# Masked cross-attention: the last key's term once per group, and weights and values as fp16 halves

## What is computed

```python
q = split_heads(layernorm(x) @ Wq + bq)        # 16 heads of 16
k = split_heads(ctx @ Wk + bk); v = split_heads(ctx @ Wv + bv)
scores = einsum('bhqd,bhkd->bhqk', q, k) / sqrt(16)
scores = where(mask > 0, -1e9, scores)         # mask is 1 on valid keys
p = softmax(scores)                            # over 257 keys
x = x + einsum('bhqk,bhkd->bhqd', p, v) @ Wo + bo
```

## Time and profile before

| | |
|---|---|
| median of 3 runs | 3067.11 us (3064.57 to 3067.53) |
| the profiled execution's own time | 3058.71 us |
| its span, first to last instruction | 3056.9 us |
| PE / DVE / ACT / POOL busy, share of the span | 86% / 66% / 59% / 54% |
| mean granted TensorE clock | 0.926 |

### The profile page before, as it was taken

One profiled execution on the slowest core, in us unless ns is written; L12 is line 12 of the kernel. 1 busy time (PEld: TensorE's weight loads), 2 busy tenths in 40 slices (PEclk: granted clock), 3 DMA queues, 4 the chain that ended last, 5 costly groups with the idle time before them and its releaser, 6 DMA issues. The chain is left out here.

```text
span 3056.9 us, 81164 instructions
## 1 busy us (share of the span) xinstructions
PE 2633.2 (86%) x31182; PEld 2052.3 (67%) x31182; DVE 2019.7 (66%) x4510; ACT 1814.4 (59%) x4252; POOL 1652.4 (54%) x1589
## 2 busy tenths in 40 slices
PE   2999999999985988986797999999994888527998
PEld 2888888888863655553355888888873666416776
DVE  4677777777764777776346777777766888653443
ACT  2667767667666777772345777777763666343333
POOL 3666666666635777773006666666644777142332
PEclk9999999999996999887798999999996999558999
DMA  5333332223300000000002212221200000451110
GB/s 145 85 84 85 84 82 76 75 77 84 92 28 1 1 1 1 1 1 14 16 15 84 64 49 64 64 64 49 64 18 16 2 2 2 170 181 48 38 40 26
DMA packets 120951, 160.04 MB, mean 52 GB/s; under 512 B 11456, under 2 KB 107840, under 8 KB 118400
## 3 DMA queue, kind: packets, MB, share of 16 engines
q1 hardware_dynamic: 115904, 140.28, 16.1%
q0 software_dynamic: 4672, 14.57, 1.3%
HBM read 139.99 MB, written 14.83 MB: 51 GB/s over the span
## 5 line engine op out<-in xcount | busy, mean ns | idle before, releaser
L570 ACT ACTIVATE x_prob<-x_prob,x_nm 128x257 f32<-128x257 f32 x512 | 254.5, 499 | 212.7 <-DVE x_nm L656 212.7
L1894 DVE TENSOR_TENSOR_SCAN m_s<-m_a,m_psD 128x1024 f32<-128x1024 f32 x128 | 284.9, 2267 | 3.0 <-PE m_psD L1721 2.9
L656 DVE CUSTOM_DVE_ANT_0 x_prob<-x_psS,x_masked,x_lastv 128x256 f32<-128x256 f32 x512 | 217.3, 481 | 104.0 <-PE x_psS L476 100.7
L1195 DVE SCALAR_TENSOR_TENSOR x_pTl<-x_psS,x_pTh 128x1024 f16<-128x1024 f32 x128 | 156.7, 1225 | 144.9 <-ACT x_pTh L1103 144.9
L1833 ACT ACTIVATE m_a<-m_dt,m_rate 128x248 f32<-128x248 f32 x512 | 206.9, 493 | 0.0
L2778 ACT ACTIVATE e1t_g<-e1t_psH,e1t_bias 128x128 f32<-128x128 f32 x312 | 89.2, 368 | 171.1 <-PE e1t_psH L2727 171.1
L1605 POOL TENSOR_TENSOR m_s<-m_s 128x1024 f32<-128x1024 f32 x64 | 150.6, 2354 | 68.5 <-DVE m_s L1894 68.5
L883 POOL TENSOR_TENSOR x_qbdh<-x_qh,all_mask4h 128x1024 f16<-128x1024 f16 x32 | 60.6, 1894 | 215.8 <-DVE x_ql L1176 215.8
L1116 ACT ACTIVATE x_vh<-x_psV 128x512 f16<-128x512 f32 x128 | 76.4, 597 | 134.4 <-PE x_psV L922 134.4
L875 POOL TENSOR_TENSOR x_ctxl<-x_ctx,x_ctxh 128x512 f16<-128x512 f32 x128 | 149.7, 1170 | 10.7
L318 POOL TENSOR_TENSOR x_ctxl<-x_ctx,x_ctxh 128x512 f16<-128x512 f32 x128 | 148.3, 1159 | 10.7
(11 more groups left out here) (591 smaller groups left out, 10617.9 us busy)
## 6 DMA issues: line engine op xcount, KB each, us to landing
x_ctx<-in_ctxT SPq DMA_DIRECT2D x64, 1024.0 KB, 6.2
x_mraw<-in_mask SPq DMA_DIRECT2D x128, 128.5 KB, 6.0
x_vxr<-x_vx SPq DMA_DIRECT2D x32, 512.0 KB, 6.9
e1r_stage<-in_L_ffn_w SPq DMA_DIRECT2D x16, 1024.0 KB, 5.0
e_rows<-e1r_pad POOLq DMA_DIRECT2D x1, 5070.0 KB, 19.6
e1t_row<-e_rows SPq DMA_DIRECT2D x39, 130.0 KB, 2.1
all_xres<-in_x SPq DMA_DIRECT2D x1, 4096.0 KB, 14.4
x_vxr<-x_vx SPq DMA_DIRECT2D x128, 32.0 KB, 3.5
```

What stands on the lines that cost most here:

```text
L570: last = act.activation(prob[b % NP][:, s, :], prob[b % NP][:, s, :], ACT.Exp, bias=nm[b % NP][:, s:s + 1], scale=-1.0, accum_out=sm[b // ...
L656: dve.tensor_tensor_reduce(prob[b % NP][:, s, 0:LAST], psS[:, s * LAST:(s + 1) * LAST], masked[g % 2][:, j, :], -SC, lastv[g % 2][:, j, s: ...
L1195: dve.scalar_tensor_tensor(pT[c % 4][1][:].rearrange("p r k n -> p (r k n)"), psS[c % 2][:], PS, pT[c % 4][0][:].rearrange("p r k n -> p ( ...
L1894: dve.tensor_tensor_scan(states, rates, psD[at % 2][:], 0.0, ALU.mult, ALU.add).then_inc(scan_done, 1)
```

## The change

Values and weights are written as fp16 pairs: ACT takes the high halves (`hi_v`; `hi_pT` now takes all 1024 columns of `psT`, scaled by `PS` = 4096), DVE the low halves (`lo_v`, `lo_pT`), which read both PSUM and the high half. `lo_v(b-1)` stands at the head of DVE's slot, `lo_pT(b-1)` where `take_pT(b-1)` stood. `attend` makes three fp16 products in place of one fp32 product. The last key's term leaves `attend`: POOL only sets its weights aside (`take_last`), spreads a group's weights in a second instruction like the one for the sums (`lasts`), PE sums them over heads in `denominators`, and DVE multiplies by the last key's values (`vx`, now transposed and kept in SBUF) and adds, in `normalise`. The DRAM round trip of those values and its broadcast loads are gone. Declarations, renames of semaphores and the unchanged surroundings are left out:

```diff
 sync
-            def load_vx(g):
-                wait(sync, pv_last, (g - 1) * GB)
-                src = vx_dram[g * GB:(g + 1) * GB, :].rearrange("(a j) n -> a j n", a=1).to_broadcast([P, GB, D])
-                sync.dma_start(vxr[g % 2][:], src).then_inc(vxr_in[g % 2], 16)
 gpsimd
-            def value_last(b):
-                g, j = b // GB, b % GB
+            def take_last(b):
                 pool.wait_ge(exp_done, b + 1)
-                pool.wait_ge(vxr_in[g % 2], 16 * (g // 2 + 1))
-                wait(pool, pv_mm, b - 2)
-                pool.tensor_tensor(pv32[b % 3][:].rearrange("p (c r n) -> p c r n", c=C, r=RG),
-                                   vxr[g % 2][:, j, :].rearrange("p (c r n) -> p c r n", c=C, r=RG),
-                                   strips(prob[b % NP][:, :, LAST]).unsqueeze(3).to_broadcast([P, C, RG, 64]), ALU.mult)\
-                    .then_inc(pv_last, 1)
+                pool.tensor_copy(plast[b // GB % 2][:, b % GB, :], prob[b % NP][:, :, LAST]).then_inc(taken, 1)
 
             def spread_sums(g):
                 pool.wait_ge(share_done, g + 1)
...
+                pool.wait_ge(taken, (g + 1) * GB)
+                pool.tensor_tensor(lasts[:], eye_q[:].unsqueeze(1).unsqueeze(1).to_broadcast([P, 4, GB, T]),
+                                   plast[g % 2][:].rearrange("p j s -> p s j").unsqueeze(3).to_broadcast([P, 4, GB, T]),
+                                   ALU.mult).then_inc(lasts_done, 1)
...
-                batch(value_last, b - 1)
+                batch(take_last, b - 1)
 tensor
             def denominators(g):
                 pe.wait_ge(sums_done, g + 1)
+                pe.wait_ge(lasts_done, g + 1)
                 wait(pe, q_lo, min(g + 3, NT))
-                for r in range(RG):
-                    last = pe.matmul(psA[64 * r:64 * r + 64, :], head_rows[:],
-                                     sums[:, 2 * r:2 * r + 2].rearrange("p c j t -> p (c j t)"), start=True, stop=True)
+                for to, src in ((0, sums), (256, lasts)):
+                    for r in range(RG):
+                        last = pe.matmul(psM[64 * r:64 * r + 64, to:to + 256], head_rows[:],
+                                         src[:, 2 * r:2 * r + 2].rearrange("p c j t -> p (c j t)"), start=True, stop=True)
...
-                wait(pe, v_out, b)
+                wait(pe, v_lo, b)
...
             def turn(b):
                 pe.wait_ge(exp_done, b + 1)
-                wait(pe, pt_first, b)
-                wait(pe, pt_second, b)
+                wait(pe, pt_lo, b)
...
             def attend(b):
-                pe.wait_ge(v_out, b + 1)
-                pe.wait_ge(pt_first, b + 1)
-                pe.wait_ge(pt_second, b + 1)
-                pe.wait_ge(pv_last, b + 1)
+                pe.wait_ge(v_lo, b + 1)
+                pe.wait_ge(pt_lo, b + 1)
...
-                        for r in range(RG):
-                            s = r * C + c
-                            pe.matmul(psO[64 * r:64 * r + 64, to:to + P],
-                                      V[b % NV][:, kt, c * P + 64 * r:c * P + 64 * r + 64], pT[b % NW][:, kt, s * P:(s + 1) * P],
-                                      start=b % 2 == 0 and kt == 0 and c == 0, stop=False, skip_group_check=True)
-                for c in range(C):
-                    to = (c * 2 + b % 2) * P
-                    for r in range(RG):
-                        last = pe.matmul(psO[64 * r:64 * r + 64, to:to + P],
-                                         pv32[b % 3][:, c * P + 64 * r:c * P + 64 * r + 64], con["ident"][:],
-                                         start=False, stop=True, skip_group_check=True)
+                        for v, p in ((0, 0), (0, 1), (1, 0)):
+                            for r in range(RG):
+                                s = r * C + c
+                                last = pe.matmul(psO[64 * r:64 * r + 64, to:to + P],
+                                                 V[b % NV][v][:, kt, c * P + 64 * r:c * P + 64 * r + 64],
+                                                 pT[b % NW][p][:, kt, s * P:(s + 1) * P],
+                                                 start=b % 2 == 0 and kt == 0 and c == 0 and (v, p) == (0, 0),
+                                                 stop=kt == 1 and (v, p) == (1, 0), skip_group_check=True)
 scalar
-                act.activation(pT[b % NW][:, 0, :], psT[:, 0:512], ACT.Copy).then_inc(pt_first, 1)
+                act.activation(flat(pT[b % NW][0]), psT[:], ACT.Copy, scale=PS).then_inc(pt_hi, 1)
 vector
-            def take_pT(b):
-                dve.wait_ge(t_mm, b + 1)
+            def lo_pT(b):
+                dve.wait_ge(pt_hi, b + 1)
                 wait(dve, pv_mm, b - NW + 1)
-                dve.tensor_copy(pT[b % NW][:, 1, :], psT[:, 512:1024]).then_inc(pt_second, 1)
+                dve.scalar_tensor_tensor(flat(pT[b % NW][1]), psT[:], PS, flat(pT[b % NW][0]), ALU.mult, ALU.subtract)\
+                    .then_inc(pt_lo, 1)
...
+            def lo_v(b):
+                dve.wait_ge(v_hi, b + 1)
+                wait(dve, pv_mm, b - NV + 1)
+                dve.tensor_tensor(flat(V[b % NV][1]), psV[:], flat(V[b % NV][0]), ALU.subtract).then_inc(v_lo, 1)
...
                 dve.wait_ge(o_ext, 2 * g + 2)
+                dve.wait_ge(vx_done, 1)
+                dve.tensor_tensor(term[:].rearrange("p c j t -> p (c j) t"), psM[:, 256:512].rearrange("p (n t) -> p n t", t=T),
+                                  vx[:, g].rearrange("p c j -> p (c j)").unsqueeze(2).to_broadcast([P, C * GB, T]), ALU.mult)\
+                    .then_inc(term_done, 1)
+                dve.wait_ge(term_done, g + 1)
                 row = oT[g % 2][:].rearrange("p c j t -> p (c j t)")
+                dve.tensor_tensor(row, row, term[:].rearrange("p c j t -> p (c j t)"), ALU.add).then_inc(term_added, 1)
+                dve.wait_ge(term_added, g + 1)
                 dve.tensor_tensor(row, row, psA, ALU.mult).then_inc(o_norm, 1)
...
+                batch(lo_v, b - 1)
                 batch(minima, b)
...
-                batch(take_pT, b - 1)
+                batch(lo_pT, b - 1)
```

More of the change, by code:

```diff
@@ L202, in masked_attention @@
         (kxp,) = parts("kx", [P, C, RG, NB], 1)
-        vx32 = sb("vx32", [P, D], F32)
-        vxr = [sb(f"vxr{n}", [P, GB, D], F32) for n in range(2)]
+        vx = sb("vx", [P, NT, C, GB], F32)
         mraw = sb("mraw", [P, GB, S2], I32)
@@ L212, in masked_attention @@
         qbd = parts("qbd", [P, C, GB, 4, T], 2)
-        K, V = parts("k", [P, C, LAST], NK), [sb(f"v{n}", [P, 2, D], F32) for n in range(NV)]
+        K, V = parts("k", [P, C, LAST], NK), parts("v", [P, 2, D], NV)
         prob = [sb(f"prob{n}", [P, 4, S2], F32) for n in range(NP)]
@@ L216, in masked_attention @@
         sm = [sb(f"sm{n}", [P, GB, 4], F32) for n in range(2)]
-        pT = [sb(f"pT{n}", [P, 2, 512], F32) for n in range(NW)]
-        pv32 = [sb(f"pv32_{n}", [P, D], F32) for n in range(3)]
-        sums = sb("sums", [P, 4, GB, T], F32)
+        pT = parts("pT", [P, 2, 512], NW)
+        plast = [sb(f"plast{n}", [P, GB, 4], F32) for n in range(2)]
+        sums, lasts = sb("sums", [P, 4, GB, T], F32), sb("lasts", [P, 4, GB, T], F32)
+        term = sb("term", [P, C, GB, T], F32)
         oT = [sb(f"oT{n}", [P, C, GB, T], F32) for n in range(2)]
@@ L230, in masked_attention @@
         ctx_in, mask_in = [sem(f"ctx_in{n}") for n in range(2)], sem("mask_in")
-        vx_out, vxr_in = sem("vx_out"), [sem(f"vxr_in{n}") for n in range(2)]
         last_hi, last_lo, kx_mm, kx_hi, kx_lo, vx_mm, vx_done = (sem(k) for k in (
@@ L238, in masked_attention @@
         sx_mm, last_done, placed = sem("sx_mm"), sem("last_done"), sem("placed")
[L239 to L242, removed]
+        k_mm, k_hi, k_lo, v_mm, v_hi, v_lo = (sem(k) for k in ("k_mm", "k_hi", "k_lo", "v_mm", "v_hi", "v_lo"))
+        s_mm, s_min, exp_done, t_mm, pt_hi, pt_lo = (sem(k) for k in ("s_mm", "s_min", "exp_done", "t_mm", "pt_hi", "pt_lo"))
+        taken, pv_mm, o_part, o_ext = sem("taken"), sem("pv_mm"), sem("o_part"), sem("o_ext")
+        lasts_done, term_done, term_added = sem("lasts_done"), sem("term_done"), sem("term_added")
         sums_done, sum_mm, share_done, o_norm, ob_ready, ob_hi, ob_lo = (sem(k) for k in (
@@ L297, in _ @@
             load(1)
[L298 to L301, removed]
             for g in range(1, NT):
@@ L305, in _ @@
                 load_mask(g)
-                load_vx(g)
         @block.gpsimd
@@ L398, in last_keys @@
                 last.then_inc(kx_mm, 1)
-                products(psV[:, 0:D], [part(lastp, lambda x: x[:, cc, :]) for cc in range(C)],
-                         [part(W["v"], lambda w: w[:, cc, :]) for cc in range(C)]).then_inc(vx_mm, 1)
+                for h in range(C):
+                    last = products(psV[:, h * NB:(h + 1) * NB],
+                                    [part(W["v"], lambda w: w[:, cc, h * P:(h + 1) * P]) for cc in range(C)],
```

(20 more changed lines are left out.)

5 lines of the change are left out of this document (1 added, 4 removed).

## The result

The changed kernel takes 3127.12 us (median of 6 runs, 3124.45 to 3129.90), the kernel before beside it 3064.76: ratio 1.021, interval 1.019 to 1.023. The profiled execution of the changed kernel took 3129.79 us, its span is 3128.0, and the mean granted clock 0.924.

The account below looks back on a forecast made before the run. PE bound the kernel before; afterwards a ring through ACT and DVE would, at 27.4 us a group against 26.25: +37 us over 32 groups, +1 at the end, 3097 on the profiled execution, 3105 as median, range 3062 to 3143.

Parts of the forecast that it names:

- a ring through ACT and DVE: Each slot runs minima, exponentials, `hi_pT`, `lo_pT`, `lo_k`, `lo_v`, next minima; bare ring 6.08 us, above PE's 6.02.
- j=2: Slot j=2: 6.53 us, from the 6.08 ring plus 0.45 for a later `hi_pT`; `normalise`, 1.2 us, hidden under the wait.
- j=3: Slot j=3: 6.52 us; ACT's `hi_v` ends 5.9 us after the minima, then `lo_v`; DVE alone 6.41.
- slots that differ otherwise: Sign of being wrong: slots differing from each other otherwise than the forecast 7.4, 6.9, 6.5, 6.5 us.
- PE's savings: PE: 0.67 us less per slot in `attend`, 0.5 a group more for `denominators`; own work 24.1 us a group.
- DVE's full list at j=0: Slot j=0: DVE's own instructions fill 7.45 us, against 6.70 before, with no gap left.
- The ring at j=1: Slot j=1: 6.08 us ring plus `lo_q` 0.52 and `ln` 0.32, together 6.92 us.
- the 4.60 us: Slot j=0 on DVE: time from the minima to the take of `psT`, the first term of the 7.45 us.
- the cover of 0.7 us: PE: transposes there at 1.8 us after the minima, before `hi_pT` wants them at 2.50; where it fails, the slot grows.
- PE keeps ahead: PE's transposes are ready before `hi_pT` wants them, and its 6.02 us a slot lie inside 6.85.
- Rival 4: PE's single buffers come free later; transposes miss the 2.50 us in every slot by 0.25 to 0.3: 3140 us, chance 0.07.
- The clock: PE in the layer's stretch: about 88% busy at granted clock 1.00; the rival of a lower clock had chance 0.06.

Follow-up runs that it names:

- term_psum: Changed kernel with the last key's term written back into PSUM, so the add of `normalise` reads one PSUM operand: 3113 us, 1.016 of the kernel before.
- turn_early_psum: `term_psum` with, on PE alone, `turn(b-1)` moved right behind `scores(b)`: 3098 us, 1.012 of the kernel before.
- lo_v_gap: Changed kernel with `lo_v(b-1)` moved behind `minima(b)` on DVE: 3117 us, 1.018 of the kernel before.
- balanced: `turn_first` with the term in PSUM and `to_add` moved on DVE from j=0 to j=3: 3007.34 us, again 3001.03; 0.981, 0.980 of the kernel before.
- fp32_balanced: Changed kernel without halves (fp32 values and weights, old PE order), term in PSUM, `to_add` moved to j=3: 3015 us, 0.984 of the kernel before.
- turn_first: Changed kernel with `turn(b-1)` right behind `scores(b)` on PE and `hi_pT(b-1)` ahead of `exps(b)` on ACT: 3056 us, 0.998 of the kernel before.

## Why the prediction was right

The forecast was slower, 3105 us in 3062 to 3143, by a ring through ACT and DVE that starts where DVE begins to wait for ACT's high half. The measured 3127 lies inside, the sign is right, and the experiments that cut the rings gave the time back without removing an instruction. The mechanism is right at j=0 and j=1 and incomplete at j=2 and j=3. The prediction named slots that differ otherwise as a sign of being wrong, and j=2 is that: 7.29 for 6.5, longer than j=1, and without the wait for `hi_pT` that the list had there. Step by step:

- PE's savings: right. `attend` 0.79, the doubled `denominators` +0.44 for the 0.5 taken. The saving is off the path, since PE has 29 us of gaps in 200. `denominators` are not wholly off it: they stand ahead of the transposes at j=2.
- DVE's full list at j=0: right, 7.44 for 7.45, though about 0.82 us of it is the step held up beside GpSimd, which came along unseen in the 4.60 us from the earlier trace rows. The ring at j=1: right, 6.89 for 6.92, with DVE's wait at 1.84 us for 1.9.
- j=2: wrong by 0.76 us, the largest miss, 24 of the missing 30 us. The step that failed is the pricing of `normalise` from the width of `lo_xn`: 1.2 us for three steps, said to be hidden. They take from 505.19 to 507.15, 1.96. The nearest row, that of `lo_xn`, had an operand in PSUM; the add has none, and I did not look for a row of that kind. `term_psum` shows the size, 17.6 us of the 24. The other 0.22 us a group are transposes that come later than the 0.45 added for them: `hi_pT` starts 3.18 us after the minima and not 2.95. Without that delay (`turn_early_psum`) j=2 is still 6.60, because the rest of DVE's list was counted low as well: the three extracts take 1.21 us (503.98 to 505.19) and not 1.03.
- j=3: wrong by 0.20 us, 6 us in all. I counted keys and `turn` on PE ahead of `hi_pT` and forgot `last_scores` between them: keys start at 509.29, the transposes at 511.24 and not at 510.6. The `hi_pT` that was to start 2.50 us after the minima starts at 2.69, so the cover of 0.7 us did not exist there.
- "PE keeps ahead", with a cover of 0.7 us: wrong. At j=2 and j=3 the transposes are late, and `lo_v_gap` shows that in j=1 the second ring lies only 0.13 us below the first, and there it ate most of a repair of the first. What the group puts on PE ahead of the transposes (`queries`, `denominators`, `last_scores`) was left out or counted low.
- Rival 4, the transposes late in every slot, 28.5 us a group and 3140 us, lies nearer to the measured 28.34 and 3127 than my own 27.4 and 3105 do. Its mechanism is there in two slots of four, but hidden behind the slow add in one of them. Most of the closeness comes from the add, which the rival did not have.
- GpSimd: the second spreading takes 1.59 us and not the 1.08 of the first. In `balanced`, where no VectorE instruction on the masks runs beside it, it takes 1.08. No engine waited for it.
- The clock: right, 1.00 from 200 to 800 us. The weight loads of 64-column tiles hid: `attend` takes the 0.79 us of the earlier trace rows here too.
- What stays open: the later layers were 3.5 us longer in this profile and 10.6 in that of `fp32_balanced` (3021.4 - 863.6 against 3056.9 - 909.7), with the same code. It is no effect of the change: `balanced` and `balanced_again` are one kernel, and their later layers took 2154.9 and 2146.5 us. Why one execution differs from another is not shown.

The sum: the list gave +38 for the layer, j=2 and j=3 add 32 x 0.96 = 31, together 69; measured 67.6. That the time missed by only 22 us is in part luck. The layer missed by 30 us and the later layers added 3.5, but I had put the median 8.4 us above the profiled execution, and for the changed kernel it lies 2.7 below. This spread between executions took 11 us off the miss.

## What to carry to other kernels

Splitting an operand into a high half on one engine and a low half on the next adds more than work: it adds a wait between two queues that ran side by side, so walk round every ring that the new wait closes, with everything queued between, and then the next ring of nearly the same length, before pricing the matmuls saved. Cut such rings by the order of issue first: the same instructions in another order were 2.3% faster here (`turn_first` against the changed kernel), and moving `to_add` and mending the slow add gave another 1.6%. Price a VectorE instruction with two SBUF inputs by a row of that kind, taken while GpSimd works. Where a step takes far longer than its width explains (0.98 us for 4 values a partition), look at what GpSimd does beside it before you call a list full.

## What the runs showed of the hardware

- A 128x256 fp32 add on VectorE with both inputs in SBUF: 1.12 us beside GpSimd's `ctxl`, ending 0.28 us after it in 30 groups of 30; 0.43 without GpSimd; 0.42 beside it with one input in PSUM.
- A 128x4 step of VectorE that reads int32 in SBUF: 0.98 us beside GpSimd's spreading of the sums, ending 0.02 to 0.03 us after it in 29 groups of 29; 0.16 three slots later.
- GpSimd's spreading of the last weights: 1.59 us where VectorE's 128x1024 step on the masks starts 0.02 us ahead of it (520.37 and 520.39), 1.08 in `balanced`, where that step runs at another time.
- The granted clock stayed at 1.00 with PE busy for 86% of a 200 us stretch and in gaps of 0.67 to 1.35 us, as it had in the stretch of the earlier trace rows with PE busy for 83%.
